# One attention and mixture-of-experts layer on one core: where SyncE begins a head's weight loads among the turning transfers

## What is computed

```python
def _mxfp4_matmul(x, codes, scales, block_size=BLOCK):
    w = codes * jnp.repeat(scales, block_size, axis=0)
    return x @ w
...
q = _mxfp4_matmul(x, wq_codes, wq_scales) + bq      # k and v alike
scores = jnp.einsum('bqhd,bkhd->bhqk', q, k) / jnp.sqrt(jnp.float32(HEAD_DIM))
attn = jax.nn.softmax(scores, axis=-1)
out = jnp.einsum('bhqk,bkhd->bqhd', attn, v).reshape(B, S, NUM_HEADS * HEAD_DIM)
return _mxfp4_matmul(out, wo_codes, wo_scales) + bo
```

## Time and profile before

| | |
|---|---|
| time, median of 3 runs | 2097.92 us (2092.08 to 2099.7) |
| span of the profiled execution, first to last instruction | 2076.3 us |
| PE busy | 1970.1 us, 95% |
| DVE busy | 1759.6 us, 85% |
| POOL busy | 1525.8 us, 73% |
| ACT busy | 1417.6 us, 68% |
| the 16 turning transfers, 127 times | 2032 transfers, 2.3 us each to landing (median) |

### The profile page before, as it was taken

One profiled execution on the slowest core, in us unless ns is written; L12 is line 12 of the kernel. 1 busy time (PEld: TensorE's weight loads), 2 busy tenths in 40 slices (PEclk: granted clock), 3 DMA queues, 4 the chain that ended last, 5 costly groups with the idle time before them and its releaser, 6 DMA issues.

```text
span 2076.3 us, 33234 instructions
## 1 busy us (share of the span) xinstructions
PE 1970.1 (95%) x10926; PEld 1700.0 (82%) x10926; DVE 1759.6 (85%) x2706; ACT 1417.6 (68%) x2686; POOL 1525.8 (73%) x1317
## 2 busy tenths in 40 slices
PE   7999999999999999999999999999999999985992
PEld 5888888888888888888888888888888888875882
DVE  6888889888889889988989888988999888977554
ACT  4776767677677667776777677776777667773454
POOL 2678778787778777886878777877888777976322
PEclk9999999999999999999999999999999999996996
DMA  4667666787678767776677667765677666771453
GB/s 97 158 160 181 163 162 160 162 184 162 156 165 179 171 147 174 169 165 158 149 161 173 143 153 154 173 158 139 163 166 173 147 139 147 190 177 51 133 151 104
DMA packets 238064, 322.66 MB, mean 155 GB/s; under 512 B 47686, under 2 KB 105798, under 8 KB 237894
## 3 DMA queue, kind: packets, MB, share of 16 engines
q1 hardware_dynamic: 234822, 312.15, 64.1%
q0 software_dynamic: 3072, 8.39, 1.4%
HBM read 35.68 MB, written 18.35 MB: 26 GB/s over the span
## 4 chain that ended last, share of the span: by engine, by line
PE 71%; SPq 11%; POOL 5%; DVE 5%; ACT 4%; DMA 2%; issue 2%; POOLq 0%; ACTq 0%; DVEq 0%
PE ps_a L749 17%; PE ps_s L621 12%; PE ps_s L622 11%; PE ps_s L623 11%; SPq L395 9%; PE ps_a L750 8%; POOL pT_both L518 4%; PE ps_a L621 3%; PE ps_a L622 3%; PE ps_a L623 3%; ACT probs L1038 2%; DMA pT<-probs 1%; DVE part_max L1393 1%; ACT pT_both L1055 1%; DVE probs L1418 1%
## 5 line engine op out<-in xcount | busy, mean ns | idle before, releaser
L518 POOL TENSOR_TENSOR pT_both<-pT,pT_both 128x512 fp32r<-128x512 f32 x1016 | 1289.5, 1298 | 346.4 <-ACT pT_both L1055 344.1
L749 PE MATMUL ps_a<-pT_both,v_both 128*128 128x512 f32 x2048 | 746.9, 398 | 0.5 <-POOL pT_both L518 0.5
L1038 ACT ACTIVATE probs<-ps_s,shift 128x1024 f32<-128x1024 f32 x512 | 566.7, 1110 | 259.2 <-DVE shift L1402 258.9
L1055 ACT ACTIVATE pT_both<-pT 128x512 fp32r<-128x512 f32 x1016 | 605.9, 630 | 194.5 <-DMA pT<-probs 161.3
L1418 DVE STREAM_TRANSPOSE probs<-probs 128x1024 f32<-128x1024 f32 x508 | 614.4, 1229 | 63.7 <-ACT probs L1038 62.7
L1393 DVE TENSOR_REDUCE part_max<-ps_s 128x1 f32<-128x1024 f32 x512 | 612.4, 1215 | 20.0 <-PE ps_s L623 18.5
L750 PE MATMUL ps_a<-pT_both,v_both 128*128 128x256 f32 x2048 | 575.6, 281 | 0.0
L749 PEld LDWEIGHTS ps_a<-pT_both,v_both 128*128 128x128 f32 x2048 | 387.1, 189 | 86.3 <-POOL pT_both L518 1.3
L621 PE MATMUL ps_s<-kT_hi,qT_hi 128*128 128x512 f32 x1024 | 407.3, 398 | 20.0 <-ACT probs L1038 16.8
L622 PE MATMUL ps_s<-kT_lo,qT_hi 128*128 128x512 f32 x1024 | 403.4, 394 | 0.0
L623 PE MATMUL ps_s<-kT_hi,qT_lo 128*128 128x512 f32 x1024 | 402.4, 393 | 0.0
(11 more groups left out here) (202 smaller groups left out, 2621.7 us busy)
## 6 DMA issues: line engine op xcount, KB each, us to landing
pT<-probs SPq DMA_DIRECT2D x2032, 128.0 KB, 2.3
x_rows<-zeros SPq DMA_DIRECT2D x46, 128.0 KB, 2.2
xg<-x_rows SPq DMA_DIRECT2D x46, 128.0 KB, 2.1
y_rows<-y_sb SPq DMA_DIRECT2D x46, 128.0 KB, 1.9
pT<-in_L_attn_x SPq DMA_DIRECT2D x4, 512.0 KB, 5.6
codes<-in_L_attn_wk_codes SPq DMA_DIRECT2D x16, 128.0 KB, 2.4
scales<-in_L_attn_wk_scales SPq DMA_DIRECT2D x64, 32.0 KB, 3.0
codes<-in_L_attn_wo_codes SPq DMA_DIRECT2D x16, 128.0 KB, 2.3
```

Of the source, the lines that this page charges most:

```text
L518: pool.tensor_tensor(pT_lo[:, p, :].rearrange("p (i n) -> p i n", i=Q4), pT[:, s % 2, g, :, t:t + 2, :].rearrange("p i t q -> p i (t q)"), ...
L749: nc.tensor.matmul(out_both, v_hi[:, h % 2, k, :], move, start=k == 0, stop=False)
L1038: nc.scalar.activation(out, src, ACT.Exp, bias=shift[:, s % SLOTS, r:r + 1], scale=SCALE, accum_out=sums[:, s % SLOTS, r, g:g + 1])\
L1055: nc.scalar.activation(pT_hi[:, p, :].rearrange("p (i n) -> p i n", i=Q4), pT[:, s % 2, g, :, t:t + 2, :].rearrange("p i t q -> p i (t q)" ...
```

## The change

SP starts the turning transfers of a slot first, and the load of a weight behind them. The loads of a head stand at s = 0 (k of the next head), s = 2 (v of the head after it), s = 4 (q of the next head) and s = 6 (o of the next head). Before they stood ahead of the turning transfers at s = 0 (k), s = 1 (o of this head), s = 2 (v) and s = 4 (q). POOL makes o at s = 0 and k at s = 2, where before it made k at s = 1 and o at s = 2; v and q stay at s = 4 and s = 6. The number of transfers and of instructions is the same.

```diff
--- before.py
+++ after.py
@@ -394,33 +394,30 @@
                         dst = pT[32 * b:32 * (b + 1), s % 2, :, i, :, :].rearrange("p g t q -> p g (t q)")
                         sp.dma_start(dst, src[:, :, b, :]).then_inc(pT_loaded[s % 2], 16)
 
+            sp.wait_ge(w_ready["k"], 1)
+            load("o", 0)
             for n in range(HALVES):
                 h, s = divmod(n, NH)
-                more = h + 1 < H
-                if s == 0 and more:
-                    wait(sp, w_ready["q"], h + 1)
-                    if h == 0:
-                        sp.wait_ge(w_ready["k"], 1)
+                if n != LAST:
+                    turn_blocks(n)
+                if s == 0 and h + 1 < H:
+                    wait(sp, w_ready["o"], h + 1)
                     load("k", h + 1)
-                if n == 0:
-                    wait(sp, w_ready["k"], 2)
-                    load("o", 0)
-                if s == 1 and h > 0 and more:
+                if s == 2 and h + 2 < H:
                     wait(sp, w_ready["k"], h + 2)
-                    load("o", h)
-                if s == 2 and h == H - 2:
-                    wait(sp, w_ready["o"], h + 1)
+                    load("v", h + 2)
+                if s == 2 and h + 2 == H:
+                    wait(sp, w_ready["k"], h + 2)
                     load("o", h + 1)
-                if s == 2 and h + 2 < H:
-                    wait(sp, w_ready["o"], h + 1)
-                    load("v", h + 2)
-                if s == 4 and more:
-                    wait(sp, w_ready["o"], h + 1 if h + 2 < H else H)
+                if s == 4 and h + 1 < H:
                     if h + 2 < H:
                         wait(sp, w_ready["v"], h + 3)
+                    else:
+                        wait(sp, w_ready["o"], h + 2)
                     load("q", h + 1)
-                if n != LAST:
-                    turn_blocks(n)
+                if s == 6 and h + 2 < H:
+                    wait(sp, w_ready["q"], h + 2)
+                    load("o", h + 1)
                 if HALVES - NH + 2 <= n < HALVES - NH + 2 + NCH:
                     g = n - (HALVES - NH + 2)
                     rows = slice(g * TPC, (g + 1) * TPC)
@@ -549,10 +546,10 @@
 
             for n in range(HALVES + 2):
                 h, s = divmod(n, NH)
-                if s == 1 and h + 1 < H:
+                if s == 0 and h < H - 1:
+                    weights("o", h)
+                if s == 2 and h + 1 < H:
                     weights("k", h + 1)
-                if s == 2 and h < H - 1:
-                    weights("o", h)
                 if s == 4 and h + 2 < H:
                     weights("v", h + 2)
                 if s == 4 and h + 2 == H:
```

## The result

The changed kernel takes 2164.96 us (median of 4 runs, 2162.11 to 2168.85), the kernel before 2095.0 (4 runs, 2091.41 to 2099.7). The ratio is 1.0335, with a 95% interval of 1.0317 to 1.0352: 70 us slower, where 40 were forecast.

A forecast was written before the change was run, and what follows sets the result against it. PE was taken to bound the kernel. Seven odd heads losing 7.7 or 7.1 us (51.5), less 14.5 lost before, gave +37; 1 for head 0 and 2 for the old order made +40: 2097.9 + 40 = 2138 us, range 2106 to 2168.

The forecast's parts named there:

- The closed loop: SP's turning transfers, load, POOL's making and probs_lo, back to SP: closed at all four loads, 28.8 us (28.0 for o).
- S(n+2) - S(n): Time between SP's starts on the turning transfers of slots n and n+2; near 28.8 us, slots 0 to 6, odd heads.
- C: Sum of issue, load to POOL, making, eight probs_lo and engine steps: 28.8 us for k, v, q; 28.0 for o.
- R(44) - R(42): Head 5: from DVE ending slot 42's last of four transposes to the same in slot 44; 28.35 us forecast.
- slots 6 to 8 take 30.7 - 28.0 = 2.7 back: Even heads: the long last pair of slots (30.7 us) against o's 28.0 us loop recovers 2.7 us of SP's lateness.
- The lag at slot 6: SP's start on slot 6's turning transfers after DVE's last transpose there: 4.55 us in even heads, 5.9 in odd ones.
- the likeliest case: The forecast itself: seven odd heads lose time to the loop, 2138 us, own range 2112 to 2164, chance 0.70.
- The lower and upper sums, +14 and +66: Whole-kernel change with SP's issue of 16 turning transfers at 10.3 us throughout (+14) or 11.6 us throughout (+66).
- the +17 by the Trainium skill's 2.0 us: Scales landing in 2.0 us, not 3.0: loop 27.8 us, 4.8 and 4.2 us a head, +17, about 2115 us.
- A late slot 5 of its own: Odd heads: q's load (2.5 us) and the zeros (0.6) stand ahead of slot 5's turning transfers, delaying slot 7's transposes.
- The spreading wins: Rival: loads reach POOL early, only SP's order counts, 14.5 us return: 2083 us; needs loop of 26.1 or less; chance 0.12.
- PE's clock falls as well: Rival: each of 14 long stalls also costs about 2 us of PE's clock, 28 us more: 2166 us; chance 0.11.

The follow-up runs named there:

- experiment 3: Changed kernel with POOL making o, k and v one slot later (s = 1, 3, 5), q still at s = 6: 2115.57 us, ratio 1.0094.
- experiment 9: Changed kernel without the repeated loads of scales, each later load being codes only (output not the reference's): 2087.12 us, ratio 0.9961.
- experiment 4: Changed kernel with ACT taking the second high part of the next head's keys ahead of slot 6's first high part: 2140.64 us, ratio 1.0218.
- experiment 10: Changed kernel with one replicating transfer of scales per load in place of four (output not the reference's): 2162.81 us, ratio 1.032.
- the run again: The kernel before, unchanged, run again beside the follow-up runs: 2093.67 us over 8 runs, profiled span 2094.4 us.
- experiment 1: Changed kernel with each load put ahead of its slot's turning transfers again, new slots and POOL order kept: 2087.72 us, ratio 0.9965.
- experiment 6: Changed kernel with POOL making o, k and v one slot later and ACT taking the next head's keys first: 2085.97 us, ratio 0.9968.

## Why the direction was right and the size was not

**The closed loop** is shown. S(n+2) - S(n) in odd heads is 28.9 (k), 28.7 (v) and 28.8 us (q) on the mean, where C was 28.8. In head 5 R(44) - R(42) is 27.4 (28.35 forecast), and the head lasts 114.2 from R(40) to R(48), where 114.5 were forecast. POOL idles ahead of q in 15 waits, 4.9 us each, and ahead of v in 8, 5.8 us each (2 to 5 forecast). Experiments 3 and 9 open the loop in two ways and odd heads fall to 761.6 and 751.3. In the changed kernel with the keys ahead (experiment 4), the order costs 38.1 us in odd heads (800.0 - 761.9) and 1.7 in head 0: this is the 40 of the forecast, with its base of 747.6 + 14.5 = 762.1 for the odd heads before.

**The step that failed** is "slots 6 to 8 take 30.7 - 28.0 = 2.7 back": there I let the pair of slots 6 to 8 take the lag back at no cost. The lag at slot 6 was about right, 4.0 us on the mean in even heads (4.55 forecast) and 6.2 in odd ones (5.9), but it is paid for there. I had followed the landing only to the exponentials. In ACT's order the second half of the next head's keys stands behind slot 6's landing as well. ACT in the changed kernel, at the end of head 5:

```profile
721.91 1.12 ACT L1085 ACTIVATE kT_hi<-ps_s,bias_k 128x1024 fp32r<-128x1024 f32 x1 [0.82 <-PE ps_s L620]
725.86 0.63 ACT L1052 ACTIVATE pT_both<-pT 128x512 fp32r<-128x512 f32 x1 [2.32 <-DMA pT<-probs]
726.40 1.10 ACT L1085 ACTIVATE kT_hi<-ps_s,bias_k 128x1024 fp32r<-128x1024 f32 x1
```

DVE, next:

```profile
727.53 1.28 DVE L1487 SCALAR_TENSOR_TENSOR kT_lo<-ps_s,bias_k,kT_hi 128x1024 fp32r<-128x1024 f32 x1 [3.18 <-ACT kT_hi L1085]
```

Slot 46's landing comes at 725.86, the second `kT_hi` right behind it, then `kT_lo`, then PE's scores of slot 48. R(48) - R(46) is 34.2 us in this head, not the 32.2 of the forecast. Before, PE waited for `kT_lo` once, 1.1 us in all, and that at 33 us, at the start of head 0, never at a border between heads:

```profile
PE ps_s L621 <- DVE kT_lo L1490: 1.1, 1, 1.1
```

In even heads a lag of 3.4 to 3.6 us at slot 6 went with a pair of slots 6 to 8 that is 0.5 to 0.65 us longer than 30.7, one of 4.4 to 4.5 with 2.0 to 2.6 us; by that, an estimate, the cover ends near 3. The price is the 24 us of experiment 4; by heads it is 9.1 in odd heads (809.1 - 800.0), 12.8 in even ones (844.7 - 831.9), 1.6 in head 0. Together with the loop's own 38.1 and 1.7, less 0.3 in even heads (831.9 - 832.2), that is 63.0; 0.9 more lie ahead of head 0, and the attention grew by 63.9. The second half is 2.1 longer and the medians are 4 further apart than the two profiled executions; that lies within the scatter of the runs.

**What was luck.** The measured time lies within the 2106 to 2168 of the forecast, but just above the likeliest case's own 2112 to 2164. It is inside only by the room left above for PE's clock, and the clock cost at most 7 us. The lower and upper sums, +14 and +66, and the +17 by the Trainium skill's 2.0 us, also leave out the 1 for head 0 and the 2 for the old order that the +40 has; with them they are +17, +69 and +20. The Trainium skill, DMA: Bandwidth & Descriptors, section Anatomy of one DMA, gives this fixed cost for transfers that GpSimd issues, and SyncE issues these; no run has a loop of 27.8 us, so that sum stays untested.

**The smaller steps.**
- *"even ones still 118.4"* failed with it: 120.7 on the mean. The prediction itself named even heads that grow as a sign of error.
- *PE's wait for the exponentials "up from 16.8 to about 50 us"* failed: 21.3. The lateness reaches PE by three ways of about 21 us each. The second, PE waiting in slot n's values for POOL's `pT_both`, is the same loop seen from its other side; I had not named it.
- *A late slot 5 of its own* (R(7) by S(5)): the mean lag at slot 5 was 5.4 us in odd heads. In experiment 10 it is 3.9, and odd heads are as long, so in the changed kernel less of this lateness gave nothing back. Nor do the zeros show: odd heads with them (1, 3 and 5) last 114.2 us on the mean, those without 116.6, where 114.5 and 113.9 were forecast. What slot 5 costs with the keys ahead stays open.
- *The 21.6 us outside the span* are not there: in the changed kernel the time is 1.7 above the span (2162.11 and 2160.4). The first profiled execution of the kernel before had a short second half, 250.9 us against 271 to 279 in the others, and PE's waits for ACT's `y_sb` are 1.6 us in it against 17.8 in the run again. The forecast is untouched, since it added a difference to the median.
- *The spreading wins*: not in the changed kernel, but its condition, a loop of 26.1 us or less, is what experiment 9 made (25.6 to 26.0 us): 2087 us, where the rival said 2083, and 7.5 us under the kernel before, where it said 14.5.
- *PE's clock falls as well*: in part. Beside one fall in the first 25 us, which all have, the granted clock fell to half 6 times in the attention of the changed kernel, 3 times in experiment 4, twice in the kernel before. One of the six, by windows of 2 us:

```profile
848.00:850.00 2.00, 0.00 (x0) 0.00 (x0) 0.96 (x1) 1.53 (x3) 0.56 (x1) 1.00 0.44 107
...
852.00:854.00 2.00, 2.00 (x10) 1.90 (x9) 1.96 (x5) 0.28 (x1) 2.00 (x2) 0.50 0.90 206
```

and PE's instructions there:

```profile
850.38 0.50 PE L618 MATMUL ps_s<-kT_hi,qT_hi 128*128 128x512 f32 x1 [2.69 <-DVE kT_lo L1487]
...
853.13 0.63 PE L746 MATMUL ps_a<-pT_both,v_both 128*128 128x512 f32 x1
...
855.53 0.39 PE L618 MATMUL ps_s<-kT_hi,qT_hi 128*128 128x512 f32 x1
```

PE idled 2.69 us for the keys, the clock then went from 2.4 to 1.2 GHz for about 3.4 us, and a matmul of 512 columns took 0.63 us instead of 0.39 to 0.40. Each fall costs at most half of its stretch, 1.7 us, so four more cost at most 7, not 28. The count and the cost of the falls are read from the traces alone; this part lies within the 24 and the 38 above, not beside them.
- *A change of under 0.5% cannot be told from none*: with ten runs it can. The interval of experiment 1 is 0.9952 to 0.9978.

## What to carry to other kernels

Where a load stands behind other transfers in one queue and its consumer stands ahead of the work for which the queue waits next, add up the whole circle (issue, landing, making, work) and hold it against the pace of the bound engine: a circle of 28.8 us against 25.2 cost 40 us here, one of 26 nothing. A single such circle of 28.8 cost nothing either where a long pair of slots came next and nothing else stood behind the late landing (experiment 6). Then follow a late landing to everything that stands behind it in each engine's order, and not only to the consumer that you think of; a pair of slots with slack for one may have none for another. A load either is begun well ahead (experiment 1) or is used well behind (experiment 6); both were faster than the kernel before by 0.3%, and which of the two hardly mattered. Used well behind also took the keys ahead in ACT's order; without that it was 0.9% slower (experiment 3).

## What the runs showed of the hardware

A transfer that replicates one row of the scales to 128 partitions (128 KB) landed in 4.8 us, the codes of the same size in 2.5, and a row to 32 partitions (32 KB) in 2.9 (3.0 before), or in 1.9 for o: time to landing did not go by bytes, and one large replicating transfer was no quicker than four small ones begun one after the other. And the 6 falls of the granted clock in the attention of the changed kernel each stood in or just behind an idle time of PE of 1.6 to 2.8 us, but they are only 6 against the 65 waits of the three rows on PE at the top.
